# Cross-attention with a gated FFN on one core: other banks for a pair's first scores, bias additions moved into the softmax stage, and a second queue for weight loads

## The reference, cut to what matters

```python
x = x + xattn(layernorm(x), ctx, ctx)        # 16 batches, 128 tokens, 512 features, all float32
x = x + ffn(layernorm(x))

def xattn(q, k, v):                          # 32 query heads on 8 key/value groups, head size 16
    qh = split(q @ Wq.T, 32); kh = repeat(split(k @ Wk.T, 8), 4); vh = repeat(split(v @ Wv.T, 8), 4)
    attn = softmax(einsum('bhqd,bhkd->bhqk', qh, kh) / 4)
    return join(einsum('bhqk,bhkd->bhqd', attn, vh)) @ Wfc.T + bfc

def ffn(x):                                  # hidden 2048; _qdot casts both sides to float8 e4m3
    gate, ff = _qdot(x, w_gating[0]), _qdot(x, w_gating[1])
    return _qdot(gelu(gate) * ff, w_linear)
```

## Time and profile before

| what | us |
|---|---|
| median of three runs | 511.97 |
| the profiled execution, its own time | 515.16 |
| its span, from the first to the last instruction | 513.3 |
| PE busy in it | 447.7 |
| start, up to the first `scores_t` | 47.4 |
| pair 0, up to the first `scores_t` of pair 1 | 59.1 |
| pair 2, likewise | 55.9 |
| last pair and tail | 67.6 |

### The profile page before, as it was taken

The page is one execution under the profiler, slowest core; times in us unless marked ns, Lnnn a source line. Parts: engine busy times, 40 slices in busy tenths (PEclk is TensorE's granted clock), DMA queues, the critical chain, the costliest instruction groups (busy, mean ns, idle before and its releaser), DMA issues.

```text
span 513.3 us, 11714 instructions
## 1 busy us (share of the span) xinstructions
PE 447.7 (87%) x4592; PEld 354.1 (69%) x4592; DVE 351.8 (69%) x694; ACT 308.2 (60%) x570; POOL 230.9 (45%) x221
## 2 busy tenths in 40 slices
PE   0865885799899998999899989999899989998997
PEld 0823773676678777777678768877677767756874
DVE  3576756598669757976679755976689675756442
ACT  4364762677437973597438863697458753686441
POOL 5144852559322861377124842277126832085000
PEclk9965787889899999999899998999999999999999
DMA  7799247644240246005600354015600332000001
GB/s 263 256 328 304 70 155 188 156 152 123 89 98 3 65 125 144 4 18 150 146 20 4 79 145 108 3 28 143 163 3 3 104 80 67 3 23 23 1 22 43
DMA packets 21912, 50.07 MB, mean 98 GB/s; under 512 B 5216, under 2 KB 5728, under 8 KB 21856
## 3 DMA queue, kind: packets, MB, share of 16 engines
q1 hardware_dynamic: 21856, 49.30, 34.2%
HBM read 23.86 MB, written 4.19 MB: 55 GB/s over the span
## 4 chain that ended last, share of the span: by engine, by line
PE 62%; DVE 15%; issue 7%; SPq 7%; DMA 3%; POOL 2%; ACT 2%; POOLq 0%; DVEq 0%; ACTq 0%
PE bank L580 16%; PE bank L600 10%; PE bank L401 7%; PE bank L403 6%; PE bank L402 6%; PE bank L498 5%; DVE mneg L956 4%; PE bank L465 4%; SPq L318 3%; PE bank L429 2%; DVE prod L1012 2%; SPq L329 2%; PE bank L516 2%; PE bank L518 2%; POOL plo L1154 2%
## 5 line engine op out<-in xcount | busy, mean ns | idle before, releaser
L1154 POOL TENSOR_TENSOR plo<-p,phi 128x512 f16<-128x512 f32 x128 | 152.3, 1201 | 75.0 <-ACT phi L767 74.2
L580 PE MATMUL bank<-x2T,wgate 128*128 128x128 fp8e4 x2048 | 138.0, 228 | 0.8 <-ACT x2T L779 0.8
L580 PEld LDWEIGHTS bank<-x2T,wgate 128*128 128x128 fp8e4 x2048 | 125.0, 102 | 13.3 <-issue 8.5
L764 ACT ACTIVATE p<-bank 128x512 f32<-128x512 f32 x128 | 77.6, 606 | 37.1 <-PE bank L498 36.5
L956 DVE TENSOR_REDUCE mneg<-bank 128x4 fp32r<-128x512 f32 x128 | 85.0, 687 | 17.9 <-PE bank L465 17.5
L465 PE MATMUL bank<-kmask,cq 128*128 128x512 f32 x128 | 64.8, 522 | 25.3 <-DVE mneg L956 22.1
L767 ACT ACTIVATE phi<-bank 128x512 f16<-128x512 f32 x128 | 77.3, 604 | 0.0
L600 PE MATMUL bank<-wlin,act 128*128 128x512 fp8e4 x256 | 73.7, 383 | 0.0
L786 ACT ACTIVATE gate<-bank 128x512 bf16<-128x512 f32 x64 | 38.2, 597 | 47.7 <-PE bank L580 32.7
L790 ACT CAST ff<-bank 128x512 bf16<-128x512 f32 x64 | 37.5, 586 | 48.7 <-PE bank L580 48.6
L498 PE MATMUL bank<-qs,ks 98*128 98x512 f32 x128 | 54.8, 428 | 7.8 <-DMA qs<-mrow 6.2
(11 more groups left out here) (101 smaller groups left out, 792.0 us busy)
## 6 DMA issues: line engine op xcount, KB each, us to landing
qs<-cq SPq DMA_DIRECT2D x96, 128.0 KB, 2.5
stage<-in_w SPq DMA_DIRECT2D x16, 512.0 KB, 5.4
ks<-khl SPq DMA_DIRECT2D x96, 64.0 KB, 2.0
xr<-in_x SPq DMA_DIRECT2D x16, 256.0 KB, 3.0
cin<-in_ctx SPq DMA_DIRECT2D x8, 512.0 KB, 4.5
out<-xr SPq DMA_DIRECT2D x16, 256.0 KB, 2.5
raw<-in_w SPq DMA_DIRECT2D x4, 512.0 KB, 7.1
kmask<-khl SPq DMA_DIRECT2D x32, 64.0 KB, 2.0
```

The costliest lines, as they stand in the source:

```text
L580: mm = pe.matmul(out[:, h * SEQ:(h + 1) * SEQ], wgate8[:, UH * v + h, kk, part, :], x2T[:, b % NB, kk, :], start=kk == 0, stop=kk == KT - 1)
L764: act.activation(p32[:, e % P32BUF, :], T[n % 2][:, :], ACT.Exp, scale=QUARTER).then_inc(p32_ok, 1)
L1154: pool.tensor_tensor(plo[:, e % PBUF, :], p32[:, e % P32BUF, :], phi[:, e % PBUF, :], ALU.subtract).then_inc(plo_ok, 1)
```

## The change

1. **Score banks.** For pairs q of 1 and more, the first scores go into banks that are idle then: two for q = 1 (T0, T1), three for later pairs (G1, T0, T1). For later pairs the first is issued in slot 15. DVE takes their maxima at the front of slots 16 to 18 (17 and 18 for q = 1), and the other early maxima in front of the FFN stage's first unit. The next users of G1, T0 and T1 (`up`, `turn_out`, `project_out`) wait for these maxima. In the start the scores of pair 0 go round six banks.
2. **Bias additions.** `add_bias(q, i)` moves to slots 5 and 8 of the softmax stage; those of pair 0 to slots 2 and 4.
3. **Queues.** ACT issues the context of pair 1 and the nine chunks 5 to 13; SP's queue keeps the rest, and `stack_max(0, 0)` stands in the middle of the query stacking.
4. **Own buffer.** The normed input of pair 0 goes to the second half of `ks`, so it is transposed first; the context of pair 1 waits for the value projection, no longer for the queries.
5. Smaller moves: in the start, the low parts of `wv` and `wfc` go from DVE to POOL; the clamped gate chunks are now 5 to 9; DVE converts gate chunks in eleven slots of pair 0 (`DVE_SLOTS`); the chain of batch 0 is one slot earlier at its start and two at its end.

```diff
-W_PLACE = ["q0", "q1", "q2", "q3", "st0", "st1", "st2", "x4", "x6", "p0", "p1", "p2", "g0", "g1"]
+W_PLACE = ["q0", "q1", "q2", "q3", "st0", "p0", "p1", "p2", "st1", "st2", "x4", "x6", "g0", "g1"]
-W_CLAMPED = [c for c in range(W_GATE, CHUNKS) if c in (5, 6, 7, 9, 11) or W_LIN <= c < W_LIN + 4]
+W_CLAMPED = [c for c in range(W_GATE, CHUNKS) if c < W_GATE + 5 or W_LIN <= c < W_LIN + 4]
-DVE_EARLY = 4
+DVE_SLOTS = ((2, 3, 4, 5, 7, 8, 10, 11, 12, 13, 15), (1, 3, 5, 7))
-S_EARLY = {16: 1, 17: 2, 18: 2}
+S_EARLY = {True: {16: 1, 17: 1, 18: 2}, False: {15: 1, 16: 1, 17: 1, 18: 2}}
+M_EARLY = {True: {17: 1, 18: 1}, False: {16: 1, 17: 1, 18: 1}}
+EARLY_BANK = {True: ("T0", "T1"), False: ("G1", "T0", "T1")}
+BIAS_SLOT = (5, 8)
+BIAS_SLOT_0 = (2, 4)
-CHAIN_E = {True: dict(turn=12, project=(13, 14, 15, 16), residual=17, rstd=15, norm=18, turn2=19),
+CHAIN_E = {True: dict(turn=11, project=(12, 12, 13, 13), residual=14, rstd=14, norm=15, turn2=17),
...
@@ scores
-                take_bank("S", q, i, s)
+                name = early_bank(q, i, s)
+                if name == "G1":
+                    pe.wait_ge(x2T_ok, NB * (q - 1))
+                elif name:
+                    pe.wait_ge(phi_ok, TILES * q - 1 + int(name[1]))
+                else:
+                    take_bank("S", q, i, s)
@@ turn_out
                     pe.wait_ge(phi_ok, TILES * (p + 1) - 1)
+                    if p + 1 < NP:
+                        pe.wait_ge(max_ok, early_done(p + 1, "T0"))
@@ project_out
                         pe.wait_ge(phi_ok, TILES * (b // NB + 1))
+                        if b // NB + 1 < NP:
+                            pe.wait_ge(max_ok, early_done(b // NB + 1, "T1"))
@@ up
-                    pe.wait_ge(ao_ok, SUMS * (p + 1))
+                    pe.wait_ge(ao_ok, SUMS * (p + 1) - 1 + part)
                 elif p:
                     pe.wait_ge(out_ok, up_batches(p - 1)[-1] + 1)
+                    if part and p + 1 < NP:
+                        pe.wait_ge(max_ok, early_done(p + 1, "G1"))
@@ tensor, start
+            for i in range(NB):
+                turn_x(0, i)
             project_k(0, 0, KT)
             for b in range(NB):
                 project_v(0, b)
-            for i in range(NB):
-                turn_x(0, i)
             for j in range(HPG):
                 project_q(0, j, 0, KT)
-            for s in range(SBANKS):
+                if j == 2:
+                    scores(0, 0, 0)
+                    scores(0, 0, 1)
+            for s in range(2, SBANKS):
                 scores(0, 0, s)
@@ scalar, start
+            def load_ahead(lo, hi):
+                for c in range(lo, hi):
+                    act.dma_start(chunk_place(c), w_d[c]).then_inc(chunk_in(c)[0], 16)
+            def load_ctx_ahead():
+                act.wait_ge(c_lo, 2)
+                act.dma_start(cin[:, :, :], ctx_d[1]).then_inc(c_in, 16)
...
+            square_hi(W_FC, wfc, 0)
             values_half(0)
+            load_ctx_ahead()
+            load_ahead(W_GATE, W_GATE + 3)
             values_hi(0)
+            queries_hi(0, 0)
             values_mid(0)
+            load_ahead(W_GATE + 3, W_GATE + 6)
+            queries_hi(0, 1)
             square_hi(W_FC + 1, wfc, 1)
+            load_ahead(W_GATE + 6, W_AHEAD)
...
@@ vector, softmax stage, slot n
-                    if odd and 0 <= m < SUMS:
-                        sums(p, m)
+                    if q < NP and n < SLOTS:
+                        for s in range(early, early + M_EARLY[first].get(n, 0)):
+                            maxima(q, 0, s)
+                        early += M_EARLY[first].get(n, 0)
                     for at, b in downs:
                         if n == at + GROUPS:
                             finish(b)
+                    if odd and 0 <= m < SUMS:
+                        sums(p, m)
...
-                    if q < NP:
-                        for s in range(early, early + S_EARLY.get(n, 0)):
-                            maxima(q, 0, s)
-                        early += S_EARLY.get(n, 0)
@@ gpsimd, softmax stage, slot n
+                    for i in range(NB):
+                        if q < NP and n == BIAS_SLOT[i]:
+                            add_bias(q, i)
+                        if first and n == BIAS_SLOT_0[i]:
+                            add_bias(0, i)
...
-                if q < NP:
-                    for i in range(NB):
-                        add_bias(q, i)
```

More of the change, by code:

```diff
@@ L103, in bank_sequence @@
         if q < NP:
-            seq += [("K", q), ("V", q)]
-        seq += [("M", p, 1)]
+            keys += [("K", q), ("V", q)]
+        keys += [("M", p, 1)]
         if q < NP:
-            seq += [("X", q, 0), ("X", q, 1), ("Q", q, 0), ("Q", q, 1)]
-            seq += [("S", q, i, s) for i in range(NB) for s in range(SBANKS)]
-    return {e: n for n, e in enumerate(seq)}, seq
-A_AT, A_SEQ = bank_sequence()
+            keys += [("X", q, 0), ("X", q, 1), ("Q", q, 0), ("Q", q, 1)]
+            keys += [("S", q, i, s) for i in range(NB) for s in range(SBANKS) if not early_bank(q, i, s)]
+    seq += [(key, f"A{n % 2}") for n, key in enumerate(keys)]
+    at, last, in_front = {}, {}, {}
+    for key, name in seq:
+        at[key] = name
+        in_front[key] = last.get(name)
+        last[name] = key
+    return at, in_front
+BANK_AT, BANK_USER = bank_sequence()
 def xattn_ffn_kernel(nc, x_d, ctx_d, w_d, bfc_d, out_d):
@@ L181, in xattn_ffn_kernel @@
         A, T, O, G = bank[0:2], bank[2:4], bank[4:6], bank[6:8]
+        bank_named = {f"{name}{n}": pair[n] for name, pair in (("A", A), ("T", T), ("O", O), ("G", G)) for n in range(2)}
         up_bank = [(G[0], G[1]), (O[0], O[1])]
@@ L260, in bank_free, with bank_of, early_done, project_source @@
             return mrow_ok, NB * q + key[2] + 1
-        def a_bank(*key):
-            return A[A_AT[key] % 2]
+        def bank_of(*key):
+            if key[0] == "S" and early_bank(*key[1:]):
+                return bank_named[early_bank(*key[1:])]
+            return bank_named[BANK_AT[key]]
         def m_bank(q, i):
-            return a_bank("M", q, i) if i else T[1]
+            return T[1] if q and i == 0 else bank_of("M", q, i)
+        def early_done(q, name):
+            return TILES * q + EARLY_BANK[q == 1].index(name) + 1
+        def project_source(q, part):
+            if q == 0:
+                return ks[:, 1, :, :, :].rearrange("p (u h) a n -> p u (h a) n", u=2)[:, part, :, :]
+            return cx[:, part, :, :]
         def chain_banks(b):
@@ L656, in _ @@
                     if q < NP:
-                        for s in range(early, early + S_EARLY.get(n, 0)):
+                        for s in range(early, early + S_EARLY[first].get(n, 0)):
                             scores(q, 0, s)
-                        early += S_EARLY.get(n, 0)
+                        early += S_EARLY[first].get(n, 0)
                 ups = len(up_batches(p)) * UPB
@@ L1039, in _ @@
             values_sum(0)
[L1040 to L1051 removed]
+            queries_lo(0, 0)
+            maxima(0, 0, 0)
+            maxima(0, 0, 1)
+            queries_lo(0, 1)
+            for s in range(2, SBANKS):
+                maxima(0, 0, s)
+            for s in range(SBANKS):
+                maxima(0, 1, s)
+            late = list(W_DVE)
             for p in range(NP):
@@ L1086, in _ @@
                         divide(p, m)
-                    if q < NP:
-                        for s in range(early, early + S_EARLY.get(n, 0)):
-                            maxima(q, 0, s)
-                        early += S_EARLY.get(n, 0)
-                    if p < 2 and late and n % 2 and (p or late[0] < W_LIN):
+                    if p < 2 and n in DVE_SLOTS[p]:
                         chunk(late.pop(0))
@@ L1098, in _ @@
                         out_lo(c_b)
+                    if q < NP and k == 0:
+                        for s in range(early, sum(S_EARLY[first].values())):
+                            maxima(q, 0, s)
+                        early = sum(S_EARLY[first].values())
                     if p and k == 2:
```

155 lines of the change are left out of this document (80 added, 75 removed).

## The result

The kernel after takes 480.84 us (median of 4 runs, 480.4 to 482.49), the kernel before beside it 511.79 (4 runs, 510.95 to 513.37). The ratio is 0.9398, 95% interval 0.9365 to 0.943. The forecast was 481. The profiled execution took 480.56 us with a span of 478.8 (before: 515.16 and 513.3).

A forecast was written before the change was run, and what follows sets the result against it. PE, busy for 87% of the span, was taken as the bound. From 515.16: 15.6 (pairs 1 to 6), 6 (clock), 8.5 (start), 3 (pair 0) give 482.1; less 1.1 for the lower median, 481 us. Range 471 to 495.

The forecast's parts named there:

- 21.6 forecast: Pairs 1 to 6: 15.6 us from score banks and moved bias additions, plus 6 us from the clock.
- rival E: Early scores not freed, waits for G1, T0 and T1 hold PE; only start and bias won: 501 us, chance 0.06.
- 2.6 us per pair: Pairs 1 to 6: net gain, 2.9 us of PE waits removed less 0.3 for bias additions in the softmax stage.
- the 1.5 forecast: Pairs 1, 3, 4 and 6: clock fall expected gone with the gap, 1.5 us each, 6 us in all.
- the term of 15.6: Pairs 1 to 6: net 2.6 us per pair times 6, from score banks and moved bias additions.
- The bias additions in slots 5 and 8: Softmax stage: POOL's later rstd makes the odd batch's normed rows meet a `plo`; 0.3 us per pair lost on PE.
- 8.5 forecast: Start: earlier maxima and stacking, next step (pair 1's key projection) at 39 instead of 48.0; bounds 3.4 and 12 us.
- the case that the prediction named as the one in which it is wrong: Start: the stacked maxima again take 5 us to land.
- The prediction's row against its own term: Start: DMA share 0.89; if all 14 chunks had to be through first, it would end at about 44, gaining 3.4 us.
- rival A: Loads bound the start and pair 0: start gains 3.4 us, pair 0 nothing; total 490 us, chance 0.17.
- What is late next: After the first `scores_t`: POOL's queue, whose chunk clamps precede the context's low part, ready at 39 us.
- 3 forecast: Pair 0: 6 us gained at the softmax stage's end, less later query projection and added DVE and POOL work; net 3.

The follow-up runs named there:

- low part first: Kernel after, with the low part of the turned outputs formed on DVE before the last sums and division; 485.93 us, ratio 0.9451.
- bias back: Kernel after, with the bias additions of pairs 2 to 7 again behind the rstd of the FFN stage; 489.96 us, ratio 0.9541.
- both back: Kernel after, with early-score banks and the bias additions of pairs 2 to 7 both taken back; 509.01 us, ratio 0.9913.
- banks back: Kernel after, with early scores of pairs 1 to 7 again in A0 and A1, their maxima behind sums and divisions; 507.95 us, ratio 0.9856.
- the kernel with the loads on SyncE: Kernel after, with context 1 and chunks 5 to 13 issued by SyncE before and between key stacking, not by ScalarE; 486.42 us, ratio 0.9465.
- six late: Kernel after, chunks 8 to 13 issued by SyncE behind query stacking: 484.94 us; landmarks come from the variant also turning pair 0's input late: 486.02 us.

## Why the prediction was right, and where it was not

**Pairs 1 to 6, undersized: 21.6 forecast, 25.8 measured.** The mechanism is as told: the wait at the turn is gone, the product takes 0.42 us, the clock stays up, and rival E (new waits on G1, T0 or T1) shows in none of the pairs 2 to 6. The failed term is the size of 2.6 us per pair. Idle time alone fell by 2.5 to 2.6 (3.02 to 0.44). But in pairs with the full clock PE's busy time fell too, from 52.56 to 51.57, with the same 575 or 576 matmuls. Before it is the row of pair 2 in the earlier trace rows, within 0.3 us; after:

```profile
150.83:202.84 52.01, 51.57 (x576) 41.60 (x575) 40.01 (x85) 36.43 (x70) 26.76 (x25) 1.00 0.33 83
```

That is 3.6 per pair, 1.4 for each us of idle time removed. Three comparisons have the same factor: low part first with 0.44 us of idle time less and 0.62 less in the pair, bias back with 1.1 more and 1.5 more, and both back against banks back, both at the low clock, with the same 1.1 and 1.5. So the step that failed is that the waits were priced at their idle time alone. Why PE's busy time falls along is not settled: matmuls overlap their neighbours when they follow at once (in the key projection 0.41 us each, 0.21 apart), and each stop may lose some of that, but no run isolates it.

By pair, 2 and 5, which had the full clock before, gained 3.6; 3, 4 and 6 gained 5.2, so the clock's part is 1.6 each, near the 1.5 forecast. Pair 1 gained 3.1 although its low level went too (0.96 before, 1.00 after). It has a wait of 1.1 us for normed rows that was 0.3, in a pair whose DVE still converts chunks. So with the steady pairs' 3.6 the term of 15.6 would have been 21.4, the clock 4 x 1.6 = 6.4, and pair 1 returns 2.1: 25.7, the 25.8 measured but for rounding.

**The bias additions in slots 5 and 8: 0.3 forecast, 0 measured in the kernel's own profile,** with PE never idle in that stage. The sentence that carried the 0.3 ("the normed rows of the odd batch then meet a `plo`") names the very place where the 3.60 us rows stand. Its size was wrong in kind: not a little in each pair, but nothing in most and 2.1 or 3.7 us in a few. At 7 of 60 it is 0.3 us per pair, the forecast's number by luck. The Trainium skill (SBUF — State Buffer, SBUF: two separate sides) has GpSimd's instructions and certain ones of DVE lock each other out of shared ports for the whole instruction. The trace agrees for the product, which ended 0.3 us behind the addition beside it. The 3.60 us go further: here the DVE instruction ended only behind three GpSimd instructions in a row.

**The start, oversized: 8.5 forecast, 5.6 measured, and 3.3 to 5.6 in the seven executions of the same start.** The failed step is "what must land first no longer stands behind the chunks in one queue". The maxima were issued on time, and the transfers were slow: 10.57 us to land, the case that the prediction named as the one in which it is wrong. What had been issued earlier, on either queue, still stood in front: with 3 MB fewer ahead, 2.0 us. By the Trainium skill (DMA: Bandwidth & Descriptors, Issuing engines are not separate DMA queues) the second queue saves issue time alone. The trace of the kernel with the loads on SyncE fits that: its maxima are issued 4.6 us later, and the start ends at 44.8, 0.6 to 3.0 later than in those seven. The prediction's row against its own term, with all of the 14 chunks through first, had the start end at about 44; the seven end it at 41.8 to 44.2, 43.2 in the mean. So for the start rival A was nearer (3.4 against 4.2 in the mean) than the forecast, and its other half, nothing in pair 0, was wrong.

**What is late next, wrong by an order.** POOL's clamps were named as the next bound, at 39; POOL was ready at 36.3 and the maxima at 41.8. Once these are early (34.35 with six late), POOL's order is the bound, at 45.2. So in either order the start is held by loads, and start and pair 0 together moved by 8.7 (10.5 in the kernel's second execution, which ends pair 0 at 95.9) against 11.5 forecast.

**Pair 0: 3 forecast, 3.1 measured,** and 6.7 in the kernel's second profiled execution, whose start was longer (43.6); that the first agrees so well is chance. The reason given for the lost part is there: in the chain ScalarE's cast waits for a clamp that waited for its load, as in the earlier trace rows.

```profile
84.03 1.04 POOL L1240 TENSOR_SCALAR stage<-stage 128x1024 f32<-128x1024 f32 x1 [6.59 <-DMA stage<-in_w]
85.10 1.06 ACT L753 ACTIVATE wlin<-stage 128x1024 fp8e4<-128x1024 f32 x1 [2.60 <-POOL stage L1240]
```

**The sum.** The errors of the start (2.9 too much) and of the pairs (4.2 too little) nearly cancel: 34.6 measured between the profiled executions (515.16 less 480.56), 33.1 forecast. Between the medians it is 31.0, since the profiled execution before lay 3.4 above its median and the one after at its own. The prediction took 1.1 us off for that. So the 481 against 480.84 is luck in part: its terms are off by up to 4 us.

## What to carry to other kernels

Price a wait on the bounding engine above its idle time: here each us of it cost 1.4, and where the granted clock fell behind it, about 1.6 us more for one fall. Before calling two causes dependent, compare pairs at the same clock, wait by wait: the same edit cost 9 us in one kernel and 1 in another by the medians, and 1.1 us of idle time in a pair in both. And before a small urgent transfer count the bytes issued ahead of it on every queue: a second issuing queue didn't let it pass them here.

## What the runs showed of the hardware

- A transfer of 8 KB took 10.6 to 12.0 us to land with 3 MB more issued ahead of it on another engine's queue (seven executions), 8.2 and 9.1 with half of that, and 2 us without them.
- A DVE instruction of 1.38 us took 3.60 beside three GpSimd ones, with the same 0.1 us between their starts; the outcome varied between pairs of one execution.
- After a pause of 1.38 us (and three of 0.1 to 0.2 close by) the granted clock was 0.50 for about 3 us in 13 pairs of 18. After pauses of 2.0 us it fell in 4 of 7, in one execution once and once not, at 2.4 us of idle time in both. After two of 1.2 and 0.5 us it fell in 5 executions of 13. A fall cost 1.6 us at the same idle time.
- The first `scores_t` of one and the same kernel stood at 41.8 and at 43.6 in two executions while their times were 480.6 and 481.1, since pair 0 took 55.9 and 52.4. In seven executions of the same start it stood between 41.8 and 44.2.
